# A bidirectional state-space scan: products with a spread row of C, summed over the states in PSUM

## The reference

```python
dA = jnp.exp(delta[..., None] * A)
bx = delta[..., None] * Bm[:, :, None, :] * x[..., None]
def step(h, inp):
    dAi, bxi, ci = inp
    h = dAi * h + bxi
    return (h, jnp.einsum('ben,bn->be', h, ci))
_, ys = jax.lax.scan(step, h0, (dA_t, bx_t, c_t))
y = jnp.transpose(ys, (1, 0, 2)) + Dp * x
return y * jax.nn.silu(z)
```

## Time and profile before

| | us |
|---|---|
| median of 3 runs | 4410.42 (4407.59 to 4414.86) |
| profiled execution, its span | 4422.2 |
| VectorE busy | 3788.5 (86%) |
| TensorE busy | 3604.0 (81%) |
| GpSimd busy | 3504.8 (79%) |
| ScalarE busy | 3101.8 (70%) |

### The profile page before, as it was taken

One profiled execution on the slowest core, in us unless ns is written; L12 is line 12 of the kernel. 1 busy time (PEld: TensorE's weight loads), 2 busy tenths in 40 slices (PEclk: granted clock), 3 DMA queues, 4 the chain that ended last, 5 costly groups with the idle time before them and its releaser, 6 DMA issues.

```text
span 4422.2 us, 57941 instructions
## 1 busy us (share of the span) xinstructions
PE 3604.0 (81%) x18192; PEld 2562.9 (58%) x18192; DVE 3788.5 (86%) x4688; ACT 3101.8 (70%) x5179; POOL 3504.8 (79%) x2085
## 2 busy tenths in 40 slices
PE   4767596888879887798878887798987989788877
PEld 1444454666546655567555774556655665567656
DVE  3999999898998989899898988989999898989710
ACT  4667576787767876688766887678876787668543
POOL 3898887888878888788887888878887888878611
PEclk7878697999979999899879998899998999889988
DMA  6233142556435663357433674345743565336555
GB/s 196 91 107 104 69 150 75 191 183 214 155 104 172 205 210 130 105 182 245 153 124 131 197 238 147 125 151 194 230 141 107 179 220 188 130 113 204 167 167 182
DMA packets 375805, 705.06 MB, mean 159 GB/s; under 512 B 31937, under 2 KB 205514, under 8 KB 371530
## 3 DMA queue, kind: packets, MB, share of 16 engines
q1 hardware_dynamic: 363210, 667.79, 46.0%
q0 software_dynamic: 12288, 33.57, 2.3%
HBM read 529.82 MB, written 171.44 MB: 159 GB/s over the span
## 4 chain that ended last, share of the span: by engine, by line
DVE 29%; PE 25%; POOL 16%; issue 15%; ACT 11%; DMA 3%; SPq 1%; DVEq 0%; POOLq 0%; ACTq 0%
DVE h L1396 10%; POOL drive L1895 9%; DVE h L1393 7%; DVE y L1405 6%; PE h_t L1170 5%; PE side L1204 4%; PE side L1341 4%; PE side L1333 3%; ACT decay L1610 2%; POOL y L1913 2%; POOL xs_dram L1970 2%; DMA expert_w<-in_w 1%; PE side L1318 1%; DVE stats L1450 1%; POOL work L1982 1%
## 5 line engine op out<-in xcount | busy, mean ns | idle before, releaser
L1895 POOL TENSOR_TENSOR drive<-xu,b_row 128x1024 f32<-128x1024 f32 x960 | 2262.7, 2362 | 386.5 <-DVE h L1396 238.8
L1610 ACT ACTIVATE decay<-delta,neg_a 128x512 f32<-128x512 f32 x2048 | 1401.8, 692 | 747.0 <-DVE h L1396 424.5
L1170 PE MATMUL h_t<-ident,h 128*128 128x128 f32 x8192 | 1332.0, 301 | 523.4 <-DVE y L1405 253.4
L1170 PEld LDWEIGHTS h_t<-ident,h 128*128 128x128 f32 x8192 | 1060.1, 155 | 979.1 <-DVE y L1405 373.1
L1405 DVE SCALAR_TENSOR_TENSOR y<-h_t,c_col,y 128x512 f32<-128x512 f32 x1488 | 1085.9, 730 | 54.0 <-PE h_t L1170 52.9
L1913 POOL TENSOR_TENSOR y<-y,scaled 128x512 f32<-128x512 f32 x496 | 631.8, 1274 | 119.4 <-ACT scaled L1631 118.4
L1396 DVE TENSOR_TENSOR_SCAN h<-decay,h,drive 128x512 f32<-128x512 f32 x512 | 654.1, 1278 | 38.6 <-ACT decay L1610 18.6
L1396 DVE TENSOR_TENSOR_SCAN h<-decay,drive 128x512 f32<-128x512 f32 x512 | 622.0, 1215 | 71.9 <-ACT decay L1610 45.8
L1393 DVE TENSOR_TENSOR_SCAN h<-decay,h,drive 128x512 f32<-128x512 f32 x448 | 573.1, 1279 | 44.7 <-ACT decay L1610 23.1
L1393 DVE TENSOR_TENSOR_SCAN h<-decay,drive 128x512 f32<-128x512 f32 x448 | 544.5, 1215 | 76.4 <-POOL drive L1895 55.7
L1204 PE MATMUL side<-prep_work,conv_diag 128*128 128x512 f32 x960 | 460.9, 605 | 27.3 <-DMA prep_work<-xz_dram 19.3
(11 more groups left out here) (205 smaller groups left out, 4355.7 us busy)
## 6 DMA issues: line engine op xcount, KB each, us to landing
expert_w<-in_w SPq DMA_DIRECT2D x350, 512.0 KB, 4.5
b_row<-b_dram SPq DMA_DIRECT2D x240, 512.0 KB, 4.2
x_dram<-xu SPq DMA_DIRECT2D x16, 2048.0 KB, 7.6
delta_dram<-prep_work SPq DMA_DIRECT2D x64, 512.0 KB, 2.9
delta<-delta_dram SPq DMA_DIRECT2D x64, 512.0 KB, 4.9
ys_dram<-work SPq DMA_DIRECT2D x40, 512.0 KB, 6.5
work<-xs_dram SPq DMA_DIRECT2D x38, 512.0 KB, 4.4
h<-in_w SPq DMA_DIRECT2D x34, 512.0 KB, 5.5
```

Source lines behind the costliest of these rows:

```text
L1170: t = pe.e.transpose(h_t[i % N_H_T][:, c * P:(c + 1) * P], its_h[:, c, :], ident[:, :])
L1610: act.e.activation(decay[:, i % N_DECAY, :], delta[:, c, its], ACT.Exp, scale=neg_a[:, c, w % 2, n:n + 1]).then_inc(decay_made, 1)
L1895: op = pool.e.tensor_tensor(drive[:, k % N_DRIVE, :], xu[:, w % 2, c, :], b_row[:, row % N_B_ROW, :], ALU.mult)
```

## The change

The states are no longer turned. A row of C is spread over the partitions by a DMA, as B is, and `multiply` makes prod = h * c_row, 128x512 with both operands in SBUF: for chunks 0 to 2 on VectorE, for chunk 3 on GpSimd (`POOL_CHUNKS`). TensorE adds each product to one of four PSUM banks `y_sum` (one for each chunk) with an identity product that accumulates over the 16 states, and ScalarE copies the sum out once for each chunk and half (`keep_y`). In the backward direction the accumulation begins with y of the forward one. The decay ring lies in SBUF (four places), with a ring of eight h and one of four prod. The two banks of side work become four. Every direction is done by halves of the tokens, with `carried_h` between them (`keep_h`). GpSimd makes the drive of two chunks and one half at a time, again 128x1024. y keeps the channels on the partitions, so `y_turn` becomes one identity product; the turning and copying of C (`c_turn`, `c_copy`) go, B and C are stored together, and the DMAs of rows have half the columns. The places of all side work and the order of SP's queue are written anew (not shown).

```diff
-N_DECAY = 3
+N_DECAY = 4
 N_DRIVE = 3
-N_B_ROW = 2
-N_H_T = 3
-N_SIDE = 2
+N_B_ROW = 3
+N_C_ROW = 3
+N_H = 8
+N_PROD = 4
+N_SIDE = 4
 N_EW = 3
-N_SCALED = 2
 TOP = 2
-POOL_TILES = (2, 6, 10, 14)
+POOL_CHUNKS = (3,)
...
+        scans = sb("scans", [P, N_H + N_PROD + N_DECAY, BANK])
...
+        h, prod, decay = scans[:, 0:N_H, :], scans[:, N_H:N_H + N_PROD, :], scans[:, N_H + N_PROD:, :]
...
-        decay = ctx.enter_context(nc.psum_tensor("decay", [P, N_DECAY, BANK], F32))
-        h_t = [ctx.enter_context(nc.psum_tensor(f"h_t{i}", [P, ED], F32)) for i in range(N_H_T)]
+        y_sum = [ctx.enter_context(nc.psum_tensor(f"y_sum{c}", [P, BANK], F32)) for c in range(EC)]
...
+            def add_product(i):
+                w, part, n, c = step_of(i)
+                pe.wait_ge(ident_set, 2)
+                if by_pool(i):
+                    pe.wait_ge(pool_multiplied, pooled_to(i))
                 else:
+                    pe.wait_ge(multiplied, multiplied_to(i))
+                if n == 0:
+                    if w or part:
+                        pe.wait_ge(y_kept, kept_to(w, part, c) - EC)
+                    if w % 2:
+                        pe.e.matmul(y_sum[c][:, :], ident[:, :], y[:, c, tokens_at(w, part)], start=True, stop=False)
+                pe.e.matmul(y_sum[c][:, :], ident[:, :], prod[:, i % N_PROD, :], start=(n == 0 and w % 2 == 0),
+                            stop=(n == N - 1)).then_inc(added, 1)
...
+                back = slice(None, None, -1 if w % 2 else 1)
+                dve.e.tensor_tensor_scan(h[:, i % N_H, back], decay[:, i % N_DECAY, back],
+                                         drive[:, i // NH % N_DRIVE, i % NH, back],
+                                         carried_h[:, n, c:c + 1] if part else 0.0, ALU.mult, ALU.add
+                                         ).then_inc(scanned, 1)
+
+            def multiply(i):
+                g = i // EC
+                dve.wait_ge(c_row_in[g % N_C_ROW], 16 * (g // N_C_ROW + 1))
+                dve.wait_ge(scanned, i + 1)
+                if i >= N_PROD:
+                    dve.wait_ge(added, i - N_PROD + 1)
+                dve.e.tensor_tensor(prod[:, i % N_PROD, :], h[:, i % N_H, :], c_row[:, g % N_C_ROW, :], ALU.mult
+                                    ).then_inc(multiplied, 1)
...
             for s in range(plan.first, plan.end):
+                if 0 <= s < NS:
+                    scan(s)
+                if 0 <= s - 1 < NS and not by_pool(s - 1):
+                    multiply(s - 1)
                 for piece, index in plan.of("dve", s):
                     side_piece(piece, index)
...
+            def keep_h(w, n):
+                first = step_at(w, 0, n, 0)
+                act.wait_ge(scanned, first + EC)
+                edge = 0 if w % 2 else BANK - 1
+                act.e.copy(carried_h[:, n, :], h[:, first % N_H:first % N_H + EC, edge]).then_inc(h_kept, 1)
+
+            def keep_y(w, part, c):
                 b, d = divmod(w, 2)
+                act.wait_ge(added, step_at(w, part, N - 1, c) + 1)
+                if b and not d:
+                    act.wait_ge(y_dumped[part], 16 * b)
+                act.e.copy(y[:, c, tokens_at(w, part)], y_sum[c][:, :]).then_inc(y_kept, 1)
...
+                if k >= N_DRIVE:
+                    pool.wait_ge(scanned, NH * (k - N_DRIVE + 1))
+                pool.wait_ge(done["u_mul"], nth("u_mul", w, c + NH - 1))
+                pool.e.tensor_tensor(
+                    drive[:, k % N_DRIVE, :, :], xu[:, w % 2, c:c + NH, tokens_at(w, part)],
+                    b_row[:, g % N_B_ROW, :].rearrange("p (a t) -> p a t", a=1).to_broadcast([P, NH, BANK]),
+                    ALU.mult).then_inc(drive_made, 1)
...
             for s in range(plan.first, plan.end):
-                k, odd = divmod(s, 2)
-                if not odd and 0 <= k + 2 < NU:
+                k, into = divmod(s, NH)
+                if not into and 0 <= NH * (k + 2) < NS:
                     feed_drive(k + 2)
-                i = s - 2 * EC - 1
-                if 0 <= i < NW * TILES and by_pool(i) and not is_first(i):
-                    pool_tile(i)
+                i = s - 2
+                if 0 <= i < NS and by_pool(i):
+                    multiply(i)
```

More of the change, by code:

```diff
@@ L799, in mamba_moe @@
         delta = sb("delta", [P, EC, L])
-        h = sb("h", [P, 2, EC, L])
-        b_row = sb("b_row", [P, N_B_ROW, L])
-        drive = sb("drive", [P, N_DRIVE, L])
-        scaled = sb("scaled", [P, N_SCALED, ED])
+        scans = sb("scans", [P, N_H + N_PROD + N_DECAY, BANK])
+        b_row = sb("b_row", [P, N_B_ROW, BANK])
+        c_row = sb("c_row", [P, N_C_ROW, BANK])
+        drive = sb("drive", [P, N_DRIVE, NH, BANK])
         conv_diag = sb("conv_diag", [P, TAPS, P])
-        y = sb("y", [P, TB, ED])
+        y = sb("y", [P, EC, L])
         xn_t = sb("xn_t", [P, DC, L])
         dbc = sb("dbc", [NP + 1, L])
-        c_col = sb("c_col", [P, 2, TB, N])
         xn2_t = sb("xn2_t", [P, DC, L])
@@ new lines, in step_of, with tokens_at, loads_into, kept_to @@
+        def step_of(i):
+            g, c = divmod(i, EC)
+            w, (part, n) = g // (NH * N), divmod(g % (NH * N), N)
+            return w, part, n, c
+        def tokens_at(w, part):
+            s = NH - 1 - part if w % 2 else part
+            return slice(s * BANK, (s + 1) * BANK)
+        def loads_into(k, ring, total):
+            return (total - k + ring - 1) // ring
+        def kept_to(w, part, c):
+            return (w * NH + part) * EC + c + 1
+        def h_kept_to(w, n):
+            return w * N + n + 1
@@ L1037, in chan_col @@
         def chan_col(d, c, k):
             return chan_sb[:, c, d * NCH + k:d * NCH + k + 1]
-        def is_first(i):
-            return i % (2 * TILES) < TB
         def by_pool(i):
-            return i % (2 * TB) in POOL_TILES or is_first(i)
-        of_vector = list(accumulate(not by_pool(i) for i in range(NW * TILES)))
-        of_pool = list(accumulate(by_pool(i) and not is_first(i) for i in range(NW * TILES)))
-        def summed_to(i):
-            return of_vector[i]
+            return i % EC in POOL_CHUNKS
@@ L1607, in feed_decay @@
                 if i >= N_DECAY:
-                    before, its_r = divmod(i - N_DECAY, NH)
-                    act.wait_ge(scanned if its_r else first_scanned, before + 1)
-                act.e.activation(decay[:, i % N_DECAY, :], delta[:, c, its], ACT.Exp,
+                    act.wait_ge(scanned, i - N_DECAY + 1)
+                act.e.activation(decay[:, i % N_DECAY, :], delta[:, c, tokens_at(w, part)], ACT.Exp,
                                  scale=neg_a[:, c, w % 2, n:n + 1]).then_inc(decay_made, 1)
-            def keep_h(i):
-                act.wait_ge(scanned, WHOLE + (i + 1) * (EC // NH))
-                act.e.copy(carried_h[:, i, :], h_half(i)[:, :, 0]).then_inc(h_kept, 1)
@@ L2128, in transfer @@
                     if w >= 2:
-                        sp.wait_ge(delta_in[c], 16 * (w - 1))
+                        for part in range(NH):
+                            sp.wait_ge(delta_in[c][part], 16 * (w - 1))
                     sp.e.dma_start(delta_dram[w % 2, c], prep_half).then_inc(done["delta_store"], 16)
                 elif piece == "delta_load":
-                    w, c = index
+                    w, c, part = index
+                    its = tokens_at(w, part)
                     sp.wait_ge(done["delta_store"], 16 * nth("delta_store", w, c))
@@ L2150, in transfer @@
[L2150 to L2151 removed]
+                    g, = index
+                    w, part, n, _ = step_of(g * EC)
+                    sp.wait_ge(done["b_store"], 16 * nth("b_store", w))
+                    if g >= N_B_ROW:
+                        sp.wait_ge(drive_made, (g - N_B_ROW + 1) * EC // NH)
+                    sp.e.dma_start(b_row[:, g % N_B_ROW, :],
+                                   b_dram[w % 2, n:n + 1, tokens_at(w, part)].to_broadcast([P, BANK])
+                                   ).then_inc(b_row_in[g % N_B_ROW], 16)
+                elif piece == "c_row_load":
+                    g, = index
+                    w, part, n, _ = step_of(g * EC)
+                    sp.wait_ge(done["b_store"], 16 * nth("b_store", w))
+                    if g >= N_C_ROW:
+                        wait_products(sp, (g - N_C_ROW + 1) * EC - 1)
+                    sp.e.dma_start(c_row[:, g % N_C_ROW, :],
+                                   b_dram[w % 2, N + n:N + n + 1, tokens_at(w, part)].to_broadcast([P, BANK])
+                                   ).then_inc(c_row_in[g % N_C_ROW], 16)
@@ L2308, in sp_program @@
                 sp.wait_ge(x_out[k], 16 * NB)
-            for tb in range(TB):
-                sp.wait_ge(y_dumped[tb], 16 * (NB - 1))
+            for s in range(NH):
+                sp.wait_ge(y_dumped[s], 16 * (NB - 1))
         pe_program(Waiter(nc.tensor))
```

661 lines of the change are left out of this document (247 added, 414 removed), and 717 rows, old and new, of tables (AT, BANK_USE).

## The result

The changed kernel takes 6803.88 us (median of 4 runs, 6803.46 to 6807.59) against 4412.64 us for the kernel before on the same chip: 1.542 times as long (95% interval 1.540 to 1.544). The prediction was 6720 us, and the range 5750 to 7300 us.

The account below looks back on a forecast made before the run. VectorE bounded the kernel before; after the change, VectorE and GpSimd taking turns at SBUF would. 6042 us of turns + 350 of side work + 342 around the scans = 6734 us of span, so 6720 us measured; range 5750 to 7300 us.

Parts of the forecast that it names:

- The bound and its mechanism: VectorE operations with two SBUF inputs and GpSimd operations reading SBUF take turns, whole operations at a time: chance 0.80, 6720 us.
- The group: Four scans (one state, one half of the tokens, four chunks), 512 in all: 7.97 us before, 11.8 us forecast.
- M, F, S, P, S, M, F, S, M, S: Forecast order: S scan, M VectorE product, F GpSimd drive of 1024 columns, P GpSimd product of 512.
- changes of hands: Passing the shared SBUF access between VectorE and GpSimd: six in each four-scan round, some 0.03 us each.
- The holds: Time an operation's columns keep the other engine out: drive 2.18, GpSimd product 1.09, scan 1.07, VectorE product 0.53 us.
- The sum: Whole kernel: 6042 us of four-scan rounds, 350 of side work, 342 around the scans, 6734 us of span.
- What stands beside the quiet groups: Side work showing in the scans' stretch: 100 us VectorE, 140 us xu products, 110 us other GpSimd work, together 350.
- The 1985 us: TensorE's 2112 new products of 512 columns at 0.94 us each, in 4013 us of its work, forecast as hidden.
- Rival 1: Only VectorE waits, GpSimd never does: 10.1 us for four scans, 5850 us in all; chance 0.08.
- Rival 2: Scans take no turns, only products do: 8.3 us for four scans, 4830 us in all; chance 0.05.
- Rival 3: No turns at 512 columns, TensorE bounds: 4343 us without idling, about 4500 with a tenth of idling; chance 0.04.
- Rival 4: No operation's start is hidden: 12.4 us for four scans, about 7400 us; chance 0.03, shared with a queue blocking rows.

Follow-up runs that it names:

- the run without turns: Changed kernel with chunks 2 and 3 sharing a y_sum bank, and VectorE's scans and products reading one fixed PSUM bank instead of decay and c_row: 4534.9 us.

## Why the prediction was right

**The bound and its mechanism** hold. The step from small operations to large ones was the risk: 21 operations of 8 to 64 columns stood for 3584 of 512 (and four of the 21, of 8 columns, are TENSOR_SCALARs with one input, which took 1.6 to 2.0 us where the shortest took 0.17 us, so that two SBUF inputs are not the only form that waits; the prediction did not say so). The pair of runs that differ in one operand shows it for scans (1641 us) and the next for products (626 us).

**The group** was put at 11.8 us, and its order from the waits: M, F, S, P, S, M, F, S, M, S. The timeline shows exactly this order from 3017.03 on (in the short names of the prediction), and 11.60 us; 289 of the 511 distances between groups in the trace are 11.6 or 11.7 us. This is the holds and gaps alone, 5.45 + 5.87 + 0.32 = 11.64 us: the 0.18 us for changes of hands do not show. The holds of 2.18, 1.09, 1.07 and 0.53 us, taken as slopes from rows of two widths, are what is seen: 1.07 us from the end of a drive to the end of a scan, and 2.18 us for a product of GpSimd that waits for a scan (1.09 + 1.07). The start of a waiting operation is hidden, as was read from the earlier trace rows.

Two of the signs that it named came out otherwise. TensorE was to be busy for at most two thirds and is for 74%, and GpSimd was to be near full and is at 66%.

**The sum** was 6734 us for a span of 6802, and the closeness, 1%, is in part luck, since its terms miss in both directions. 512 groups at 11.6 us are 5940 us and not 6042. The scans begin at 64 us and end at 6558 us, so 308 us lie around them instead of 342. What stands beside the quiet groups comes to 6494 - 5940 = 554 us instead of 350.

What was put at nothing there is VectorE's idle time. VectorE was busy for 6168 of the 6494 us, so 326 us are idle; 134 us of that are products that wait until TensorE's sum has freed their place in the ring of prod, and 99 us are ten waits of scans, of up to 19.6 us. The trace names nothing that ended the ten, but the longest end right behind a drive that GpSimd makes late, after issuing its 16 indirect DMAs of a batch (L1954, from 2069 to 2094 us before the scan below). VectorE first, then GpSimd:

```profile
2096.18 6.80 DVE L1415 TENSOR_TENSOR_SCAN scans<-scans,drive 128x512 f32<-128x512 f32 x1 [19.01 <-issue]
```

```profile
2093.74 4.63 POOL L1886 TENSOR_TENSOR drive<-xu,b_row 128x1024 f32<-128x1024 f32 x2
2098.34 1.25 POOL L1897 TENSOR_TENSOR scans<-scans,c_row 128x512 f32<-128x512 f32 x1
2099.56 2.33 POOL L1886 TENSOR_TENSOR drive<-xu,b_row 128x1024 f32<-128x1024 f32 x1
```

The same rows show something that the theory does not have. This scan waits not for one operation of GpSimd but for three in a row, the second drive, a product and a third drive, all at full speed, and ends 1.09 us behind the last. In the whole trace 13 scans took 4.5 to 8.0 us in this way, some 50 us in all. So the turns are not strictly one instruction each; what decides when GpSimd keeps the way was not tested.

The other 554 - 326 = 228 us are side work and longer waits inside VectorE's instructions, such as these 50 us. Part of them comes from side work on GpSimd, which reads SBUF too, and takes its turns:

```profile
L1908 POOL TENSOR_TENSOR xu<-xu,prep_work 128x1024 f32<-128x1024 f32 x64 | 202.6, 3165 | 110.9 <-DVE prep_work L1457 110.9
...
L1922 POOL TENSOR_TENSOR rstd<-rstd,minus_half 128x8 f32<-128x8 f32 x21 | 49.1, 2338 | 1.6
```

The product for xu went from 2360 to 3165 ns; the small one of the norms, 2338 ns here, takes 1649 ns in the run without two SBUF inputs. How the 228 us divide between VectorE's side work and GpSimd's was not taken apart. Row loads that come late, the other thing that was costed at nothing, do not show: the trace has no wait of VectorE or GpSimd for a DMA of c_row or b_row. (The kernel before has 272 such loads of b_row, not the 256 that the prediction counts.)

**TensorE** was hidden, as said, but not at the size said: an instruction of the sums takes 734 ns on average and all of them 2560 us, where in the run without turns they take 611 ns and 1980 us. Most of the difference is the clock.

```profile
3016.03 3.79 PE L1227 MATMUL y_sum<-scans,ident 128*128 128x512 f32 x4 [2.74 <-DVE scans L1426]
```

Two products take 3.79 us here, at a granted clock of 0.50 and after 2.74 us in which TensorE was idle; in the earlier trace rows two take 1.88 us. In the trace of the changed kernel 892 of the 4096 instructions ran wholly at the lower level, with a median of 1.06 us when another stood right before them and 1.22 us when not; in the run without turns it was 100. At the higher level the medians are 0.59 and 0.70 us, so that coming one by one costs 0.1 us and the lower level 0.5 us. The 1985 us were a price for packed ones at full clock.

**The rivals.** Rival 1 (only VectorE waits) falls with GpSimd's 2.18 us product. Here the Trainium skill's page "SBUF — State Buffer", section "Who interferes with whom", which says that whoever comes second waits, is borne out by the trace for both sides; and its limit of the rule to GpSimd instructions that read SBUF agrees with the 2.33 us for two scans over memsets. Rival 2 (scans don't take the second way) is false as well; made true by force, it gave 5161 us where its price was 4830. Rival 3 (no turns), made true, gave 4535 us. The 4500 that it named do not follow from its own words: a tenth of idling on 4013 us gives 4013 x 1.1 + 330 = 4744 us. What was measured is 5%, 3964 us busy of the 4193 from 77 to 4270 us. So even without turns this way to sum the states, with the work placed as it is, was not faster than the kernel before. Rival 4 (no start is hidden) wanted 12.4 us for a quiet group and falls with the 11.6 us.

## What to carry to other kernels

Before an operand of VectorE moves from PSUM to SBUF, look whether GpSimd reads SBUF at that time; if both inputs would then lie in SBUF, the two engines' times for their columns add up, as they did here, instead of lying side by side. To price it, take the time of each at two widths, count only the columns' part of it, and write down the order that the waits force. A few tiny operations in the trace, ten times as long as their neighbours of the same shape, were the only sign of it here, and worth more than the averages.

## What the runs showed of the hardware

- `tensor_tensor_scan` takes part in the turns like a product: 1.27 us with one input in PSUM, mostly 3.4 us behind a 1024-column product of GpSimd, and up to 8.0 us behind four operations of GpSimd in a row.
- A GpSimd memset of 512 columns (525 ns) doesn't hold up a scan with two SBUF inputs.
- Operations of up to 64 columns wait as long ones do: 21 of them took over 0.4 us in the kernel before, up to 2.3 us, each ending within 0.1 us of a GpSimd product.
- VectorE's busy share can't tell work from turns: it is 92% in the changed kernel, where 1.1 us of a scan's mean of 2.39 us are waiting, and 91% with all the work on VectorE, where a scan takes 1.21 or 1.28 us.
- TensorE's granted clock had a mean of 0.98 in the stretch of the scans in the run without two SBUF inputs, nearly always the level of 2.4 GHz, with TensorE busy for 3964 of 4193 us. In the changed kernel, busy for 4813 of 6463 us, it was 0.86, so in part the level of 1.2 GHz. The columns are those of the earlier trace rows:

```profile
77.00:4270.00 4193.00, 3963.80 (x12651) 2114.27 (x12652) 3608.91 (x4548) 2754.12 (x4668) 3427.74 (x1940) 0.98 0.58 185
```

```profile
77.00:6540.00 6463.00, 4813.01 (x12647) 2305.73 (x12648) 6147.28 (x4547) 2785.64 (x4667) 4363.66 (x1940) 0.86 0.38 120
```
